# A two-layer graph attention kernel: attention begun with the first 512 tokens, the rest of the tokens prepared between its steps, the large-score test put at the end

## The reference

```python
# layer 0
qkv = layer_norm(x, g1, be1) @ w_qkv           # 8 heads of 16
scores = einsum('nhd,mhd->hnm', q, k) * SCALE
attn = softmax(where(adj != 0, scores, -inf))
x = x + einsum('hnm,mhd->nhd', attn, v) @ w_proj + b_proj
x = x + gelu(layer_norm(x, g2, be2) @ w1 + b1) @ w2 + b2
# layer 1
h = x @ Wt.T + bt
s = leaky_relu(h @ Wa.T + ba, 0.2)
w = softmax(where(adj > 0, s, NEG), axis=1)
out = layer_norm(x + (w @ h) @ Wp.T + bp) * gamma + beta
```

## Time and profile before

| | us |
|---|---|
| median of 3 runs (lowest, highest) | 1310.8 (1310.02, 1312.16) |
| the profiled execution | 1311.44 |
| its span | 1309.6 |
| busy TensorE, VectorE, ScalarE, GpSimd | 1204.3, 1128.4, 1058.1, 864.0 |
| mean granted TensorE clock | 0.971 |

### The profile page before, as it was taken

One profiled execution on the slowest core, in us unless ns is written; L12 is line 12 of the kernel. 1 busy time (PEld: TensorE's weight loads), 2 busy tenths in 40 slices (PEclk: granted clock), 3 DMA queues, 4 the chain that ended last, 5 costly groups with the idle time before them and its releaser, 6 DMA issues.

```text
span 1309.6 us, 32088 instructions
## 1 busy us (share of the span) xinstructions
PE 1204.3 (92%) x12034; PEld 349.8 (27%) x12050; DVE 1128.4 (86%) x1647; ACT 1058.1 (81%) x1201; POOL 864.0 (66%) x900
## 2 busy tenths in 40 slices
PE   5654999999999999999999999999999998998997
PEld 3330111111111111111111111111111126874443
DVE  6664999999999999999999999999999994653555
ACT  4553999999999999999999999999999993441000
POOL 5682777777777777777777777777777763440011
PEclk9875999999999999999999999999999998999999
DMA  5001332323332234223332323332233247405860
GB/s 173 1 1 51 126 119 98 114 98 121 122 114 98 98 117 142 98 98 113 113 130 99 114 98 110 121 128 97 98 116 127 83 148 263 137 1 201 292 255 25
DMA packets 41149, 152.49 MB, mean 116 GB/s; under 512 B 5216, under 2 KB 19360, under 8 KB 30752
## 3 DMA queue, kind: packets, MB, share of 16 engines
q1 hardware_dynamic: 36640, 148.26, 31.9%
q10 hardware_dynamic: 4352, 2.10, 0.5%
HBM read 110.50 MB, written 39.85 MB: 115 GB/s over the span
## 4 chain that ended last, share of the span: by engine, by line
ACT 63%; PE 19%; issue 8%; DVE 5%; POOL 3%; POOLq 0%; DVEq 0%
ACT probs L1158 37%; ACT probs L1152 26%; PE ps L786 4%; PE ps L705 2%; PE ps L775 2%; POOL probs L1059 2%; PE ps L714 2%; PE ps L1357 2%; DVE probs L1260 2%; PE ps L763 1%; DVE probs L1198 1%; DVE acc_sb L1268 1%; PE ps L808 1%; PE ps L822 1%; PE ps L679 1%
## 5 line engine op out<-in xcount | busy, mean ns | idle before, releaser
L1260 DVE SCALAR_TENSOR_TENSOR probs<-m,ps 128x512 f32<-128x512 bf16 (+1 forms) x1024 | 928.9, 951 | 36.7 <-PE ps L1357 18.5
L1158 ACT ACTIVATE probs<-probs 128x1536 f32<-128x1536 f32 x512 | 866.7, 1694 | 0.9
L1095 POOL TENSOR_TENSOR probs<-probs,m 128x512 f32<-128x512 f32 x512 | 596.0, 1164 | 229.9 <-ACT probs L1152 200.9
L1370 PE MATMUL ps<-probs,v_sb 128*17 128x512 f32 x4096 | 539.6, 599 | 0.0
L1357 PE MATMUL ps<-kq 32*128 32x512 bf16 x6144 | 427.5, 380 | 39.5 <-DVE probs L1260 9.7
L1152 ACT ACTIVATE probs<-ps 128x512 f32<-128x512 f32 x512 | 410.3, 801 | 26.9 <-PE ps L1357 26.2
L1357 PEld LDWEIGHTS ps<-kq 32*128 32x128 bf16 x6144 | 114.8, 93 | 567.4 <-ACT probs L1152 499.1
L1074 POOL TENSOR_SCALAR m<-adj_in 128x512 bf16<-128x512 int32 x256 | 157.3, 615 | 4.0 <-issue 3.9
L1370 PEld LDWEIGHTS ps<-probs,v_sb 128*17 128x17 f32 x4096 | 68.1, 95 | 217.7 <-issue 210.9
L348 POOL TENSOR_TENSOR probs<-probs,cols 128x2 f32<-128x2 f32 x16 | 11.7, 729 | 110.4 <-DVE probs L625 110.4
L423 ACT ACTIVATE probs<-ps 128x512 f32<-128x512 f32 x8 | 4.8, 597 | 84.1 <-PE ps L763 84.1
(11 more groups left out here) (134 smaller groups left out, 615.1 us busy)
## 6 DMA issues: line engine op xcount, KB each, us to landing
adj_in<-in_adj_t SPq DMA_DIRECT2D x64, 1024.0 KB, 5.7
mask_t<-m SPq DMA_DIRECT2D x64, 512.0 KB, 2.9
kq<-mask_t SPq DMA_DIRECT2D x16, 2048.0 KB, 8.2
attn_t<-acc_sb SPq DMA_DIRECT2D x16, 256.0 KB, 6.6
probs<-in_x SPq DMA_DIRECT2D x8, 256.0 KB, 4.2
tail_words<-attn_t SPq DMA_DIRECT2D x4, 512.0 KB, 3.3
adj_in<-attn_t SPq DMA_DIRECT2D x4, 512.0 KB, 4.4
out<-probs ACTq DMA_DIRECT2D x16, 128.0 KB, 3.7
```

The lines of the kernel that those rows point to most:

```text
L1095: nc.gpsimd.tensor_tensor(pr, pr, m01[:, (k // 2) % MRING, :], ALU.mult).then_inc(postmasked, 1)
L1158: nc.scalar.activation(pr, pr, ACT.Exp, scale=UNIT).then_inc(exped, 1)
L1260: nc.vector.scalar_tensor_tensor(out=pr, in0=m.to_broadcast([P, n, CH]), scalar=1.0, in1=ps[:, b:b + n, :], op0=ALU.subtract, op1=ALU.add)\
L1370: last = nc.tensor.matmul(ps[RT * hh:RT * hh + VW, 6 + g, :], v_sb[:, t, h * VW:(h + 1) * VW], probs[:, k % SLOTS, hh // 2, (hh % 2) * CH: ...
```

## The change

The preparation of a chunk no longer comes ahead of attention. Only chunk 0 is prepared first. During steps 0 to 63, in windows w of 8 steps (PREP), chunk w+1 is prepared in pieces: after S and P of step 8w TensorE transposes x of chunk w+1 and makes the values of chunk w ("turn"), after step 8w+3 the keys of w+1 ("k"), after step 8w+5 its queries ("q"). A piece uses the two PSUM banks that follow those of its step; the next step then starts on the banks of the step before (`first_bank`). S(k+1) behind a piece waits for M2(k), and S(k+2) for the engine that reads the piece (`pair_released`). The other engines have their share between their parts of the steps: ScalarE `key_high` ahead of D at o == 4 and `query_high` at 6, `norm_turned` and `values` behind R at 1, the middle parts at 5 and 7 (o is k % 8); VectorE statistics at 0, normalise at 2, key rests at 3, query rests at 5, key lows at 6; GpSimd the root at 1 and both query low parts at 0 and 3.

The squares are of the keys as packed (`k_pack`) and no longer of `k_hi`, so each key element counts once and not twice, and the limit goes from 4 to 2 times SAFE squared. They are made in steps 68 to 316, one per eight steps; the sums ("norms") are pieces after steps 98 + 32j, the last piece ("bound") after 330. The flag is read after all steps: if scores are small, the tail follows; otherwise the exact maximum, all attention again, and the tail. The barrier and branches ahead of attention are gone. x comes in three buffers; the scratch lies in `q_shift` and `tail_words`, so the tail's parameters are loaded at mask group 9. ScalarE loads its table while x is on its way.

```diff
+PREP = 2 * CH // P
-        def exact_maximum(eng, program):
-            eng.wait_ge(flag_made, 4)
-            too_large = eng.value_load(flag[0:1, 0:1], min_val=0, max_val=1)
-            with eng.If(too_large > 0):
-                program(eng)
...
+        pair_after = {}
+        for w in range(NC):
+            pair_after[PREP * w] = ("turn", w)
+            if w + 1 < NC:
+                pair_after[PREP * w + 3] = ("k", w + 1)
+                pair_after[PREP * w + 5] = ("q", w + 1)
+            pair_after[2 * NT + 4 * PREP * w + 34] = ("norms", w)
+        pair_after[2 * NT + 4 * PREP * NC + 10] = ("bound", 0)
+        first_bank = [0]
+        for k in range(2 * TLS):
+            first_bank.append((first_bank[k] + HG + (2 if k in pair_after else 0)) % 6)
+        def pair_bank(k, u):
+            return (first_bank[k] + HG + u) % 6
+        def ends(eng, tail, second):
+            eng.wait_ge(flag_made, 4)
+            small_scores = eng.value_load(flag[0:1, 0:1], min_val=0, max_val=1)
+            with eng.If(small_scores > 0):
+                tail(eng, 1)
+            with eng.Else():
+                second(eng)
+                tail(eng, 2)
...
 SyncE
             for G in range(GROUPS):
                 store_mask(G)
                 if G + 2 < GROUPS:
                     load_adj(G + 2)
+                if G + 3 < NC:
+                    load_x(G + 3)
+                if G == per_chunk + 1:
+                    sp.wait_ge(v_done, NC)
+                    sp.wait_ge(q_lo_made, 2 * NC)
+                    sp.wait_ge(k_lo_made, 2 * NC)
+                    tail_parameters(sp)
...
 GpSimd
             for k in range(TLS):
...
                 post_mask(k)
+                w, o = k // PREP, k % PREP
+                if w < NC:
+                    if o == 1 and w + 2 < NC:
+                        root(w + 2)
+                    if w > 0 and o in (0, 3):
+                        query_low(w, o // 3)
+                m = k - 2 * NT - 4
+                if m >= 0 and m % 8 == 0 and m // 8 < 4 * NC:
+                    square(m // 32, m // 8 % 4)
...
 ScalarE
             for k in range(TLS + 1):
+                w, o = k // PREP, k % PREP
+                if w + 1 < NC and o == 4:
+                    key_high(w + 1)
+                if w + 1 < NC and o == 6:
+                    query_high(w + 1)
                 if k < TLS:
                     exp_direct(k)
                 if k > 0:
                     exp_rest(k - 1)
+                if w < NC and o == 1:
+                    if w + 1 < NC:
+                        norm_turned(w + 1)
+                    values(w)
+                if w + 1 < NC and o == 5:
+                    key_middle(w + 1)
+                if w + 1 < NC and o == 7:
+                    query_middle(w + 1)
...
 VectorE
+            for k in range(TLS):
+                masks(k, 0)
+                w, o = k // PREP, k % PREP
+                if o == 0 and w + 2 < NC:
+                    statistics(w + 2)
+                if o == 2 and w + 2 < NC:
+                    normalise(w + 2)
+                if w + 1 < NC:
+                    if o == 3:
+                        key_rests(w + 1)
+                    if o == 5:
+                        query_rests(w + 1)
+                    if o == 6:
+                        key_lows(w + 1)
+                kind, j = pair_after.get(k - 1, (None, 0))
+                if kind == "norms":
+                    largest_norms(k - 1, j)
+                    if j == NC - 1:
+                        bound_columns()
+                if kind == "bound":
+                    decide(k - 1)
...
 TensorE
+            def pair_released(k):
+                kind, j = pair_after[k]
+                if kind == "turn":
+                    if j + 1 < NC:
+                        pe.wait_ge(hT_made, j + 2)
+                    pe.wait_ge(v_made, j + 1)
+                elif kind == "k":
+                    pe.wait_ge(k_rest_made, 2 * j + 2)
+                elif kind == "q":
+                    pe.wait_ge(q_rest_made, 2 * j + 2)
+                elif kind == "norms":
+                    pe.wait_ge(norms_read, j + 1)
+                else:
+                    pe.wait_ge(flag_made, 1)
...
             def scores(k, shifted):
...
+                if k - 1 in pair_after:
+                    pe.wait_ge(opened, k)
+                    pe.wait_ge(premasked, 2 * k)
+                elif k > 0:
+                    if k - 2 in pair_after:
+                        pair_released(k - 2)
                     pe.wait_ge(opened, k)
                     pe.wait_ge(premasked, 2 * k - 1)
...
+            turn_x(0, 0)
+            clear()
+            pe.wait_ge(params_in, 80)
+            project_keys(0, (2, 3))
+            pe.wait_ge(w_scaled, 1)
+            project_queries(0, (4, 5))
+            for k in range(TLS):
+                scores(k, False)
+                if k >= LEAD:
+                    products(k - LEAD)
+                if k in pair_after:
+                    pair(k)
...
+            ends(pe, tail, second)
```

More of the change, by code:

```diff
@@ L94, in gnn_kernel @@
[L94 to L100, removed]
+        q_words = q_shift[:, :, :].rearrange("p g n -> p (g n)").bitcast(F32)
@@ L1132, in values, with query_middle @@
+            def query_middle(j):
+                at = slice(j * CH, j * CH + CH)
+                for g in range(2):
+                    act.wait_ge(q_rest_made, 2 * j + g + 1)
+                    nc.scalar.activation(q_pack[:, g, 1, at], rest[:, g, :], ACT.Copy).then_inc(q_mid_made, 1)
             def values(j):
@@ L1191, in rests, with query_rests @@
+            def query_rests(j):
                 at = slice(j * CH, j * CH + CH)
                 if j > 0:
[L1193 to L1200 removed]
@@ L1202, in low_parts @@
-            def low_parts(j):
+                    dve.wait_ge(q_lo_made, 2 * j)
+                for g in range(2):
+                    b = 4 + g if j == 0 else pair_bank(PREP * (j - 1) + 5, g)
+                    dve.wait_ge(q_hi_made, 2 * j + g + 1)
+                    nc.vector.scalar_tensor_tensor(out=rest[:, g, :], in0=q_pack[:, g, 0, at], scalar=cols[:, 2:3],
+                                                   in1=ps[:, b, :], op0=ALU.mult, op1=ALU.add)\
+                        .then_inc(q_rest_made, 1)
@@ L1211, in low_parts @@
-                last.then_inc(lo_made, 1)
-            statistics(0)
-            statistics(1)
-            normalise(0)
-            dve.wait_ge(params_in, 80)
-            nc.vector.tensor_scalar(wq_sb, wq_sb, SCALE / UNIT, None, ALU.mult).then_inc(w_scaled, 1)
-            dve.wait_ge(const_made, 1)
-            for a in range(2):
-                last = nc.vector.tensor_reduce(cols[:, 2 + a:3 + a],
-                                               identf[:, :].rearrange("p (h a d) -> p h a d", h=HG, a=2)[:, :, a, :],
-                                               AX.XY, ALU.add, negate=True)
@@ new lines, in _ @@
+            statistics(0)
+            dve.wait_ge(const_made, 1)
+            for a in range(2):
+                last = nc.vector.tensor_reduce(cols[:, 2 + a:3 + a],
+                                               identf[:, :].rearrange("p (h a d) -> p h a d", h=HG, a=2)[:, :, a, :],
+                                               AX.XY, ALU.add, negate=True)
+            last.then_inc(signs_made, 1)
+            normalise(0)
+            dve.wait_ge(params_in, 80)
+            nc.vector.tensor_scalar(wq_sb, wq_sb, SCALE / UNIT, None, ALU.mult).then_inc(w_scaled, 1)
@@ L1279, in _, with second, tail @@
+            def second(dve):
+                for g in range(2):
+                    copy_acc(NC - 1, g)
+                all_reach(dve, phase)
+                maximum_vector(dve)
+                all_reach(dve, gm_phase)
+                for k in range(TLS, 2 * TLS):
+                    masks(k, TLS)
+            def tail(dve, R):
+                tail_vector(dve, R, copy_acc)
+            ends(dve, tail, second)
         @block.tensor
@@ L1302, in project_v, with project_queries @@
+            def project_queries(j, banks):
+                for g in range(2):
+                    nc.tensor.matmul(ps[:, banks[g], :], wq_sb[:, g, :], hT[:, j % 2, :], start=True, stop=True)\
+                        .then_inc(q_done, 1)
+            def project_v(j, b):
                 for s in range(SUB):
-                    last = nc.tensor.matmul(ps[:, 6, s * D:(s + 1) * D], hT[:, j % 2, s * P:(s + 1) * P], wv_sb,
+                    last = nc.tensor.matmul(ps[:, b, s * D:(s + 1) * D], hT[:, j % 2, s * P:(s + 1) * P], wv_sb,
```

517 lines of the change are left out of this document (280 added, 237 removed).

## The result

The changed kernel takes 1325.57 us (median of four, 1324.43 to 1325.89) against 1311.48 for the kernel before beside it: ratio 1.0105, interval 1.0093 to 1.0117, so slower by 14 us. 1330 was forecast.

What follows compares the result with a forecast made beforehand. ScalarE was taken to set the pace, VectorE and TensorE nearly full. The 95.4 us saved are given back within 64 steps (+1.6); 1311.4 + 1.6 + 16.3 + 1.5 = 1330.8, so 1330, range 1317 to 1342 (8 in 10: 1281 to 1346).

Steps and rivals of the forecast that it cites:

- The start: Before attention: only chunk 0 prepared, D(0) at 19.9 us in place of 115.30, 95.4 us saved.
- window 0: First eight steps of attention, preparing chunk 1: begins cold, taken as 30 us.
- window 7: Last eight of the first 64 steps: a turn of values alone, 17.6 us.
- The late pieces: After step 64: eight norms pieces losing 0.62 + 1.10 us each, the bound 2.5 more, 16.3 us in all.
- The join: Branch on the flag between the last steps and the tail: 1.5 us added, ends 0 to 13.
- The window chain: Eight steps with preparation, followed wait by wait at full clock: 26.6 us against 14.9, 11.7 lost per window.
- The clock: TensorE's waits lower its granted clock: 2 us a window, 12 for six windows; ends 0 and 6.6 a window.
- the two waits: TensorE's waits of some 2 us in each window, at D(1) and at D(7), expected to lower the clock.
- Rival A: In the windows, waits overlap better and each costs VectorE's work, 22.8 us: 1272 us in all; chance 0.33.
- The point from which it decides: Window length of 25 us: below it the kernel is faster even with the 16.3 us of late pieces.
- The range: Forecast's own 1317 to 1342 us; named ends: clock 0 to 6.6 a window, key lows 1.41 to 3.08, late pieces as drawn.

Runs made afterwards that it cites:

- the run with empty pieces: Changed kernel with the test left out but the nine late pieces kept empty in the bank rotation (no squares, products, reduce or reader wait): 1314.66 us.
- the order experiments: Changed kernel with, by run: norm_turned and values ahead of R on ScalarE, 1305.22 us; normalise earlier, 1324.96; ScalarE's order, norms by four and key lows earlier, 1280.06.
- the two runs on the test: Changed kernel with the large-score test left out, 1306.58 us, and the same with the nine late pieces kept but empty, 1314.66 us.
- the run without the test: Changed kernel with squares, norms pieces, bound piece and decision left out, the flag set at the start: 1306.58 us, ratio to before 0.9961.
- the kernel with the key lows earlier: Changed kernel with ScalarE's order, norms by four chunks, key middle parts one step earlier and key lows earlier, ahead of query rests: 1280.06 us.
- ScalarE's order: Changed kernel with norm_turned and values ahead of R, not behind it, in the second step of each window: 1305.22 us, ratio to before 0.995.
- Fillers: Six products of zeros on TensorE ahead of S in first and third steps, windows 1 to 7: 1325.26 us with normalise earlier; 1302.71 with key lows earlier.

## Why the prediction was right, step by step

The sum came within 5 us by errors that partly cancel: against the forecast of 1330.8 for the profiled execution, the start was 1.75 longer, window 0 1.6 shorter, the windows 1 to 6 7.9 shorter, window 7 1.3 longer, the late pieces 0.7 and the tail with the join 0.4 dearer.

- **The start** was sized 1.75 us too short (21.65 for 19.9). The first low part of the queries began 1.3 later than drawn (18.51), and S(0) stood 1.6 after that, at 20.13, where I had 1.15. The size of the start is not fixed either: in the run with empty pieces, which has the same start, TensorE's query products took 1.89 for 3.04 and S(0) 0.83 for 1.47, with a granted clock of 1.00 ahead of D(0) for 0.94, and D(0) came at 19.89.
- **The window chain** is the heart of the sum, and its mechanism stood. At full clock 26.6 was forecast and 26.39 measured. That the sum is so near is in part luck. Its steps, forecast and measured (window 5): 3.65 and 3.23; 4.05 and 4.10; 1.9 and 1.87; 3.8 and 4.65; 2.2 and 1.92; 3.7 and 3.86; 3.3 and 2.76; 4.0 and 4.19. The fourth was sized 0.85 too short, as I had normalise at its uncontended 1.1; the first, fifth and seventh together were 1.24 too long and made it good. Beside the 1.41 of the key lows in the earlier trace rows GpSimd was not idle, as I wrote, but on an operation of 128x4 (22.71 to 24.10); they took 2.35 here, near my 2.2. Two of the order experiments took named waits away, that behind values and that behind the key lows, and the time went with them; the third, normalise, took its wait away and gave six windows 0.9 us in all.
- **The clock** was the term that was too large. Windows 1 to 6 sum to 163.7. At full clock a window took 26.4, and the sixth, which normalises nothing, 25.6 (25.58 in the two runs on the test), 157.5 in all: 6.2 us by the clock, where I had 12. I let the waits slow half of TensorE's path at worst and took a third of it; the granted clock was 0.91 to 1.00. That it falls because of the two waits, as the prediction has it, no run shows: windows 4 and 2 have the same instructions, and ran at 1.00 and 0.91. With window 0 at 28.4 for 30 and window 7 at 18.9 for 17.6, D(64) came at 232.6, not 239.
- **The late pieces**: 16.3 forecast, 17.0 measured by two ways (stage rows, and the run without the test). The split into two waits of 0.62 and 1.10 was 0.88 and 0.98 by the steps at four pieces, and 0.88 and 1.58, less the 0.48 of the change of chunk, at four; the bound took 2.2 for 2.5. The empty pieces cost 0.80 each. The squares on GpSimd were hidden, and SP's parameters too: beside the steps behind pieces and at changes of chunk, no step of the long stage took over 2.2 us, and their mean is 1.857 for 1.859 before.
- **The join**: 1.5 forecast, 0 measured. L451, VectorE's first instruction of the tail, starts 1.73 us after D(511) began, for 1.72 before. The branch at the end costs nothing on the way into the tail. The Trainium skill (Runtime: NRT & Kernel Launch, Instruction fetch mechanics) says that code is fetched ahead in sequence and that a taken branch out of what has been fetched stalls; this row agrees with the first. A stall for the jump over the redo doesn't show: the execution is 1.8 us longer than the span, as before. The 1.94 us that the tail lost lie elsewhere in it, with a granted clock of 0.96 for 0.97; the same tail took 239.1 to 240.7 in the other runs, for 240.07 here. So the 1.5 of the sum was near for another reason than the one given.
- **Rival A** did not come about in this kernel. But its price, 22.8 us per window, was right for the kernel with the key lows earlier (22.67). The point from which it decides, 25 us a window, holds as far as it was tried: with ScalarE's order the windows 1 to 6 average 24.9, and the kernel is 6 us faster than before, with all late pieces in it. My case against A, S behind the piece in program order, turned out to be a matter of the order of a few small jobs on ScalarE and VectorE, and two runs of reordering undid it.
- **The range** of 1317 to 1342 isn't the sum of the ends that it names: a clock term of 0 to 6.6 in six windows alone spans 1318 to 1358.

What the change as a whole hides: two things were tied together. The branch ahead of attention, with the wait for the flag in front of it, cost 12.5 us, and moving it alone gets that back. The other half is to be held against that kernel, not against the one before: preparing between the steps brought D(0) 78.7 us nearer (21.65 for 100.32), the 64 steps then took 89.6 more (210.99 for 121.44), and the test's pieces 17 more. Ordered as in the run with the key lows earlier, the same preparation and two norms pieces end 18 us ahead of that kernel (1280.06 for 1298.37).

## What to carry to other kernels

Work interleaved into a pipeline is priced by the buffers it borrows, not by its own length: a piece that takes the two spare banks costs one wait even when it is empty, and a second for its reader, so here two large pieces beat eight small ones. Before giving up on such a change, find which late release each borrowed buffer waits for, and put the releasing job ahead of work that is not urgent; go on until a window is as long as the busiest engine in it. And when a change moves two things, run each alone: here the smaller one gained 1% by itself.

## What the runs showed of the hardware that was not expected

- The four small normalise operations took 1.11, 1.25, 1.53 or 2.04 us, by where GpSimd's product of 1.16 us or its mask of 0.6 us fell. A reorder on ScalarE took 0.8 us off them in the windows where they had 2.04, with no edit on either of the two engines.
- The granted clock in a first step was 0.65 in one window and 1.00 in the next of one kernel, with the same instructions in the same order (windows 2 and 3 with ScalarE's order, 4.83 and 3.23 us). Fillers that made TensorE 13% busier (23.9 for 21.1 us a window) left the clock of six windows at 0.94.
